# Values after the output rows in a local attention, and two PSUM rings in a second attention

## The chip, the cores and the metric

The kernel runs on one core of one Trainium2 chip. The metric is the device time of one execution, in microseconds. A core has five engines that run their own instruction streams and meet at semaphores: TensorE (PE: matrix products), VectorE (DVE), ScalarE (ACT), GpSimd (POOL) and SyncE (SP, which issues DMAs here). Products land in PSUM banks, and another engine has to read a bank before TensorE may form the next product in it.

## The reference

Four blocks in a row, each added to its input after a normalisation. x is 16 x 512 x 128, fp32; 8192 rows in all.

```python
x = x + _layernorm(_L0_attn_ref(_layernorm(x), w_qkv, w_out))       # local attention
x = x + _layernorm(_L0_ffn_ref(_layernorm(x), centroids, ...))      # routing, 8 experts
x = x + _layernorm(_L1_attn_ref(_layernorm(x), Wqkv, bqkv, Wout, bout))
x = x + _layernorm(_L1_ffn_ref(_layernorm(x), W1, b1, ...))

# _L0_attn_ref: 16 heads of 64, window of 32
xn = x * rsqrt(mean(x * x) + 1e-6)
q, k, v = split(xn @ w_qkv.T)
q, k = apply_rope(q), apply_rope(k)
mask = (q_pos >= k_pos) & (q_pos - k_pos <= 32)
out = softmax(where(mask, q @ k.T / 8, -1e9)) @ v @ w_out.T

# _L1_attn_ref: 16 heads of 8, all 512 positions
q, k, v = split(x @ Wqkv + bqkv)
q, k = apply_rope(q), apply_rope(k)
out = softmax(q @ k.T / sqrt(8)) @ v @ Wout + bout
```

## The kernel before

The program is a chain of stages that each cover the whole input, with every engine's instructions written out in order and semaphores between them. The change touches two stages: `l0_attention` and `l1_attention`. The time axis of the trace has the local attention up to about 1083 us, then routing, the expert layer, the second attention from about 1650 to 2660 us, and the last layer.

**Local attention.** A batch (512 rows) is 8 steps, numbered s = 0 to 7, one for each pair of heads (128 of the 1024 inner dimensions), 16 batches, 128 steps. In each step TensorE forms the projections of queries and keys for the pair (`project`, L540, three passes each, as the fp32 operands are split in a high and a low part) and one piece of the values of a coming batch (`value`, L530), from two `a_proj` banks used in turn; then the scores of the pair (`max_scores` and the shifted, turned ones, L578 to L621), and for older pairs the sums of the exponentials (L634), the weighted values (L643) and the rows of the output (`rows`, L548). Sums, reciprocal and rows work on four heads at once, so they come once in two steps: sums at the end of an odd step, rows at the start of an even one. ScalarE copies each projection out (`a_raw`, L352, and `a_v`, L334), VectorE multiplies queries and keys by the cosines (`a_qT`, `a_kT`, L477), GpSimd multiplies the swapped copy by the sines (L303) and adds (L308). VectorE also takes maxima of the scores (L493), the reciprocal of the sums (L509) and the scaling by it (L483, L514).

A bank may be written again when the semaphore `copied` says that ScalarE has read it; for values and queries the kernel also waits for `rope_done`, a count of VectorE's products. The list `uses` sets which bank each use gets. Once a batch, fixed by step offsets (LOAD_X to SUM_Y), come the statistics of the next input, its factor, its normalisation (`normalised`, L414), its turning by TensorE (`transposes`, L524), and the same for the output (`OUT_Y`, L445, and sums). The factor of a normalisation, 1/sqrt(variance + 1e-5) followed by the rms one, is formed on GpSimd by seven small operations on 128 x 4 (`factors`, `sum_factors`).

**Second attention.** One batch is a turn of 32 steps, 16 turns. Each step has one unit of scores for maxima (two matmuls, L1955, read by VectorE's `reduce_max`, L1759) and one of turned, shifted scores (two matmuls, L1973, read by ScalarE's exponential, L1688). Beside these, at fixed steps (`SLOTS`), a turn has twelve other products: `turn_in` (the normalised input turned, read by ScalarE, L1698), `q0` to `q3` (queries and keys and their swapped copies, L1916, read by VectorE, which adds the bias and multiplies by cosine or sine in one operation, L1771), `v` (L1921, bias added by VectorE, L1778), `out0` to `out3` (read by VectorE, `quotients`), `att` (L1935, read by ScalarE) and `y` (bias added by VectorE). These twelve share a ring of two double banks, `s_ps`, with the scores for maxima; the turned scores have three banks of their own, `t_ps`. GpSimd adds two products to rotated queries or keys (`wholes`, L1619).

## Time and profile before

| | |
|---|---|
| median of 3 runs | 2857.4 us (2855.66 to 2862.07) |
| the profiled execution | 2855.56 us, its span 2853.8 us |
| TensorE busy | 2106.2 us (74%) |
| VectorE busy | 2078.9 us (73%) |
| ScalarE busy | 1500.5 us (53%) |
| GpSimd busy | 1161.3 us (41%) |
| mean granted TensorE clock | 0.877 of full |

The busy shares are means over five stages. In each stage the stretch views below give the shares of that stage, and a single instruction that comes once per pair of steps or once per turn (first start, last start, count) gives the length of a pair or a turn. A timeline shows one pair, with the idle time ahead of an instruction and what ended it in square brackets.

### The profile page before, as it was taken

The numbers are of one execution on the slowest core, as the hardware profiler recorded it, in microseconds if no ns is written. First come the engines' busy times: TensorE is split into PE (matmuls) and PEld (weight loads), VectorE is DVE, ScalarE is ACT, GpSimd is POOL, SyncE is SP. The second block draws the span as 40 slices with busy tenths as digits, with TensorE's granted clock in tenths as the row PEclk, the third lists the DMA queues.
The fourth block names the chain that finished last, engine by engine and source line by source line (L and its number), as shares of the span: only waits on it lengthen the run. The fifth ranks groups of instructions, "written<-read, shape, count | busy, mean of one in ns | idle before, by whom it ended". The sixth has DMA issues, their size and how long they took to land. (4 is left out here: it accounts for less than half of the span.)

```text
span 2853.8 us, 73730 instructions
## 1 busy us (share of the span) xinstructions
PE 2106.2 (74%) x26748; PEld 1206.3 (42%) x26748; DVE 2078.9 (73%) x5353; ACT 1500.5 (53%) x2776; POOL 1161.3 (41%) x1165
## 2 busy tenths in 40 slices
PE   4898989888989987111009828888888888888597
PEld 3676767666767766100004302222322222232354
DVE  4677777776767775766417828888888888888598
ACT  4565656565656652000005406666666666667487
POOL 5677667676767770000363346311221112210122
PEclk9999999999999996555559958998999999999799
DMA  3233333332333330000022233311122111120001
GB/s 103 65 82 72 73 75 74 79 77 70 74 75 76 75 70 6 1 1 1 21 69 68 77 64 59 51 27 24 24 30 37 28 24 23 29 39 4 9 26 33
DMA packets 103685, 136.76 MB, mean 48 GB/s; under 512 B 23782, under 2 KB 78982, under 8 KB 103047
## 3 DMA queue, kind: packets, MB, share of 16 engines
q1 hardware_dynamic: 99206, 123.34, 19.6%
q0 software_dynamic: 4096, 8.40, 1.1%
q8 instruction: 232, 3.80, 0.6%
q14 instruction: 151, 1.23, 0.2%
HBM read 26.52 MB, written 12.58 MB: 14 GB/s over the span
## 5 line engine op out<-in xcount | busy, mean ns | idle before, releaser
L1759 DVE TENSOR_REDUCE d_nmax_<-d_s_ 128x2 bf16<-128x1024 f32 x512 | 619.9, 1223 | 116.3 <-PE d_s_ L1955 113.7
L1688 ACT ACTIVATE d_pT_<-d_t_ 128x512 f32<-128x512 f32 x1024 | 557.1, 598 | 243.7 <-PE d_t_ L1973 235.7
L303 POOL TENSOR_TENSOR a_other<-a_other,a_rope 128x512 f32<-128x512 f32 x256 | 322.1, 1279 | 300.6 <-DMA a_other<-a_raw 300.4
L1986 PE MATMUL d_o_<-d_pT_,d_v_ 128*32 128x256 f32 x4096 | 332.3, 410 | 0.2 <-ACT d_pT_ L1688 0.2
L1973 PE MATMUL d_t_<-d_qs_,d_ks_ 49*128 49x512 bf16 x1024 | 207.5, 402 | 84.2 <-ACT d_pT_ L1688 42.4
L371 ACT ACTIVATE a_pT<-a_t 64x384 f32<-64x384 f32 x512 | 248.2, 485 | 33.2 <-PE a_t L621 23.9
L509 DVE RECIPROCAL a_rden<-a_o 128x512 f32<-128x512 f32 x64 | 214.5, 3352 | 52.7 <-PE a_o L634 52.7
L1955 PE MATMUL d_s_<-d_ks_,d_qs_ 48*128 48x512 bf16 x1024 | 208.0, 403 | 58.3 <-DMA d_ks_<-d_part_ 29.0
L477 DVE TENSOR_TENSOR a_qT<-a_proj,a_rope 128x512 f32<-128x512 f32 x128 | 87.6, 684 | 165.4 <-ACT a_raw L352 165.3
L1188 ACT ACTIVATE c_hT_<-c_in_,c_beta_,c_gamma_ 128x512 f32<-128x512 f32 x16 | 12.4, 777 | 359.2 <-PE c_in_ L1308 359.2
L823 POOL DMA_INDIRECT sorted_x<-x_tokens,pos x64 | 61.5, 961 | 313.8 <-DVEq L720 294.6
L352 ACT COPY a_raw<-a_proj 128x512 f32<-128x512 f32 x256 | 150.6, 588 | 73.4 <-PE a_proj L540 68.7
L540 PE MATMUL a_proj<-a_xnT_hi,a_w_lo 128*128 128x512 f32 x256 | 116.8, 456 | 93.9 <-ACT a_v L334 88.0
L1973 PEld LDWEIGHTS d_t_<-d_qs_,d_ks_ 49*128 49x128 bf16 x1024 | 49.7, 93 | 316.4 <-ACT d_pT_ L1688 203.5
L358 ACT CAST a_qB<-a_qT 128x512 bf16<-128x512 f32 x128 | 79.3, 620 | 184.9 <-POOL a_qT L308 184.8
L877 PE MATMUL b_tot<-b_count,b_ones 128*128 128x3 bf16 x126 | 23.6, 187 | 201.1 <-DVE b_junk L959 189.3
L643 PE MATMUL a_o<-a_pT,a_v 128*32 128x160 f32 (+1 forms) x4096 | 168.4, 306 | 4.1 <-DVE a_oT L514 2.4
L308 POOL TENSOR_TENSOR a_kT<-a_kT,a_other 128x512 f32<-128x512 f32 x128 | 164.1, 1282 | 0.0
L308 POOL TENSOR_TENSOR a_qT<-a_qT,a_other 128x512 f32<-128x512 f32 x128 | 163.6, 1278 | 0.0
L1986 PEld LDWEIGHTS d_o_<-d_pT_,d_v_ 128*32 128x32 f32 x4096 | 90.5, 111 | 172.6 <-ACT d_pT_ L1688 90.9
L548 PE MATMUL a_y<-a_wo,a_oT 128*128 128x128 f32 x1024 | 135.2, 287 | 17.2 <-issue 16.4
L643 PEld LDWEIGHTS a_o<-a_pT,a_v 128*32 128x32 f32 x4096 | 123.9, 113 | 37.1 <-issue 21.4
(269 smaller groups left out, 4695.6 us busy)
## 6 DMA issues: line engine op xcount, KB each, us to landing
a_other<-a_raw SPq DMA_DIRECT2D x512, 128.0 KB, 2.4
d_qs_<-d_part_ SPq DMA_DIRECT2D x192, 64.0 KB
d_ks_<-d_part_ SPq DMA_DIRECT2D x192, 64.0 KB
a_xpre<-x SPq DMA_DIRECT2D x16, 256.0 KB, 2.8
a_xres<-x SPq DMA_DIRECT2D x16, 256.0 KB, 2.9
c_xs_<-sorted_x SPq DMA_DIRECT2D x16, 256.0 KB, 2.7
c_w_<-e_w SPq DMA_DIRECT2D x16, 256.0 KB, 3.2
sorted_x<-c_xs_ SPq DMA_DIRECT2D x16, 256.0 KB, 2.0
```

The lines of the kernel that those rows point to most:

```text
L303: nc.gpsimd.tensor_tensor(other[s % 2][:, side, :], other[s % 2][:, side, :], rope[:, 1, :], ALU.mult).then_inc(rope2_done, 1)
L308: nc.gpsimd.tensor_tensor(dst, dst, other[s % 2][:, side, :], ALU.add).then_inc(add_done, 1)
L352: nc.scalar.copy(raw[s % 2][:, side, :], proj[bank][:, 0:T]).then_inc(copied, 1)
L371: nc.scalar.activation(dst[rows, :, 64 * c:64 * c + HB], src[rows], ACT.Exp, scale=SCALE).then_inc(exp_done, 1)
L509: nc.vector.reciprocal(rden[:], o_ps[:, 0:T]).then_inc(rden_done, 1)
L548: ins = nc.tensor.matmul(y_ps[:, t * 128:(t + 1) * 128], oT[:, 2 * (chunk % 2) + half, t * 128:(t + 1) * 128], wo_sb[:, 2 * chunk + half, ...
L643: ins = nc.tensor.matmul(o_ps[QD * i:QD * (i + 1), 128 * t:128 * t + widths[t]], v_sb[k_v][:, t, col:col + QD], pT[k_p][i][:, BAND * t:BAN ...
L1688: nc.scalar.activation(pT[kt][pair][:, a, :], t_ps[(j + turn.k) % 3][:], ACT.Exp).then_inc(exp_done, 1)
L1759: nc.vector.reduce_max(out, bank_of(unit, e)[:], AX_X, negate=True).then_inc(read_dve, 1)
L1955: nc.tensor.matmul(bank_of(unit, e)[:, a, :], qs[e.k][rows, hp, qt * 128:(qt + 1) * 128], ks[e.k][rows, hp, :], start=True, stop=True).the ...
L1973: nc.tensor.matmul(t_ps[(2 * n + a + e.k) % 3][:], ks[e.k][rows, hp, kt * 128:(kt + 1) * 128], qs[e.k][rows, hp, :], start=True, stop=True ...
L1986: ins = nc.tensor.matmul(o_ps[HC * i:HC * (i + 1), cols], v[e.k][:, kt, g * GH + i, :], pT[kt][i // 2][:, i % 2, cols], start=(kt, half) = ...
```

## The change

**Local attention.** The order of a step on TensorE becomes queries, keys, (turned input), rows or the rest of the weighted values, values, scores; it was rows, values, queries, keys, (turned input), rest, scores. The banks of queries, keys and values follow this order in `uses`, and the bank of values now waits for the count of VectorE's products of the same step. The values of the next batch begin a step later (`V_FIRST`), the steps of loading, normalising and turning move by one, and each factor is one power on GpSimd of a number that VectorE forms from the variance with one multiply-add.

```diff
-        NCONST = 6 + 8
+        NCONST = 4 + 8
...
-        LOAD_X, STAT_X, NORM_X, TURN_X, LOW_X = -12, -8, -6, -5, -4
-        LOAD_RES, COPY_Y, STAT_Y, OUT_Y, SUM_Y = 10, 14, 15, 17, 18
-        V_FIRST = 5
+        LOAD_X, STAT_X, ROOT_X, NORM_X, TURN_X, LOW_X = -11, -8, -7, -5, -4, -3
+        LOAD_RES, COPY_Y, STAT_Y, ROOT_Y, OUT_Y, SUM_Y, ROOT_SUM = 10, 14, 15, 16, 17, 18, 19
+        V_FIRST = 6
...
-            uses += [("v", s), ("q", s), ("k", s)]
+            uses += [("q", s), ("k", s)]
             if s == TURN_X % PAIRS:
                 uses += [("xn", s)]
+            uses += [("v", s)]
...
-                n = 6 * b
                 pool.wait_ge(stats1, b + 1)
-                nc.gpsimd.tensor_tensor(ve[:], mv1[:, :, 1], eps5[:], ALU.add).then_inc(pool_step, 1)
...
-                nc.gpsimd.tensor_tensor(comb[:], rr[:], rstd[:], ALU.mult).then_inc(comb_ready, 1)
+                nc.gpsimd.tensor_tensor(comb[:], ve[:], neg_half[:], ALU.pow).then_inc(comb_ready, 1)
...
+                ins.then_inc(x_stat, 1)
+                dve.wait_ge(x_stat, 2 * b + 2)
+                nc.vector.tensor_scalar(ve[:], mv1[:, :, 1], 1.0 + 1e-6, 1e-11, ALU.mult, ALU.add).then_inc(stats1, 1)
...
-                products = 2 * (PAIRS * b + s) + (1 if what == "xn" else 0)
-                if what != "k" and (before or what == "xn"):
-                    pe.wait_ge(rope_done, products)
+                ready = {"q": 0, "k": None, "xn": 1, "v": 2 if s == TURN_X % PAIRS else 1}[what]
+                if ready is not None and (before or ready):
+                    pe.wait_ge(rope_done, 2 * (PAIRS * b + s) + ready)
...
+                if alive(0, before, left):
+                    if s == 0:
+                        pe.wait_ge(xnT_ready, b + 1)
+                    for side, what in enumerate("qk"):
+                        bank = bank_of(b, k, s, what, before, left)
+                        project(k, s, side, bank)
+                if s == TURN_X % PAIRS and formed("xn", s, left):
+                    transposes(b + 1, bank_of(b, k, s, "xn", before, left))
                 if s % 2 == 0 and alive(LAG_ROWS, before, left):
...
+                if s % 2 == 1 and alive(LAG_REST, before, left):
+                    quad, chunk = quad_of(b, s, LAG_REST)
+                    pe.wait_ge(norm_done, 2 * quad + 1)
+                    weighted_values(chunk, k if s >= LAG_REST else 1 - k, chunk % 2, 1)
                 if formed("v", s, left):
...
-                    value(kv, nv, bank)
...
+                    value(kv, nv, bank, scores_next)
```

On TensorE, an even step in the middle of the local attention, from the sums of one four-head group (`a_ones`) to the first scores. Before (`a_w_lo,a_xnT_hi` is the values' product, `a_xnT_hi,a_w_lo` a query's or key's):

```order
L634 MATMUL a_o<-a_pT,a_ones 32x128 x4
L548 MATMUL a_y<-a_wo,a_oT 128x128 [waits a_norm_done]
L548 MATMUL a_y<-a_wo,a_oT 128x128 x7
L530 MATMUL a_proj<-a_w_lo,a_xnT_hi 128x512 [waits a_rope_done,a_copied]
L530 MATMUL a_proj<-a_w_hi,a_xnT_lo 128x512
L530 MATMUL a_proj<-a_w_hi,a_xnT_hi 128x512
L540 MATMUL a_proj<-a_xnT_hi,a_w_lo 128x512 [waits a_rope_done,a_copied]
L540 MATMUL a_proj<-a_xnT_lo,a_w_hi 128x512
L540 MATMUL a_proj<-a_xnT_hi,a_w_hi 128x512
L540 MATMUL a_proj<-a_xnT_hi,a_w_lo 128x512 [waits a_copied]
L540 MATMUL a_proj<-a_xnT_lo,a_w_hi 128x512
L540 MATMUL a_proj<-a_xnT_hi,a_w_hi 128x512 [waits a_exp_done,a_max_done,a_round_done]
```

The same place now:

```order
L601 MATMUL a_o<-a_pT,a_ones 32x128 x4
L507 MATMUL a_proj<-a_xnT_hi,a_w_lo 128x512 [waits a_rope_done,a_copied,a_xnT_ready]
L507 MATMUL a_proj<-a_xnT_lo,a_w_hi 128x512
L507 MATMUL a_proj<-a_xnT_hi,a_w_hi 128x512
L507 MATMUL a_proj<-a_xnT_hi,a_w_lo 128x512 [waits a_copied]
L507 MATMUL a_proj<-a_xnT_lo,a_w_hi 128x512
L507 MATMUL a_proj<-a_xnT_hi,a_w_hi 128x512
L515 MATMUL a_y<-a_wo,a_oT 128x128 [waits a_norm_done]
L515 MATMUL a_y<-a_wo,a_oT 128x128 x7
L499 MATMUL a_proj<-a_w_lo,a_xnT_hi 128x512 [waits a_rope_done,a_copied]
L499 MATMUL a_proj<-a_w_hi,a_xnT_lo 128x512
L499 MATMUL a_proj<-a_w_hi,a_xnT_hi 128x512 [waits a_exp_done,a_max_done,a_round_done]
```

Queries and keys moved to right behind the sums, the rows behind them, and the values, which wait for `a_rope_done`, are last ahead of the scores.

On VectorE, the normalisation of the next input (`a_xpre`) among the maxima (`a_nmax`) and the reciprocal. Before:

```order
L477 TENSOR_TENSOR a_qT<-a_proj,a_rope 128x512 [waits a_copied]
L476 REGISTER_ALU
L477 TENSOR_TENSOR a_kT<-a_proj,a_rope 128x512 [waits a_copied]
L492 ISA [waits a_st_done]
L493 TENSOR_REDUCE a_nmax<-a_s 128x4 [waits a_s_done]
L492 REGISTER_ALU
L493 TENSOR_REDUCE a_nmax<-a_s 128x4 [waits a_s_done]
L414 TENSOR_SCALAR a_xpre<-a_xpre,a_mv,a_comb 128x128 [waits a_comb_ready]
L414 TENSOR_SCALAR a_xpre<-a_xpre,a_mv,a_comb 128x128 x3
```

The same operation now:

```order
L460 TENSOR_REDUCE a_nmax<-a_s 128x4 [waits a_s_done]
L381 TENSOR_SCALAR a_xpre<-a_xpre,a_mv,a_comb 128x128 [waits a_comb_ready]
L381 TENSOR_SCALAR a_xpre<-a_xpre,a_mv,a_comb 128x128 x3
L475 REGISTER_ALU [waits a_den_done]
L476 RECIPROCAL a_rden<-a_o 128x512 [waits a_norm_done]
L443 REGISTER_ALU [waits a_st_done]
L444 TENSOR_TENSOR a_qT<-a_proj,a_rope 128x512 [waits a_copied]
```

The normalisation moved from an even step, where no reciprocal follows in the step, to an odd one, where the reciprocal and the product of the queries stand directly behind it.

**Second attention.** The shared ring is split by reader. `s_ps` keeps the scores for maxima and `out0` to `out3`, which VectorE reads; `t_ps`, three banks, takes the turned scores and `turn_in`, `q0` to `q3`, `v`, `att` and `y`, which ScalarE reads. ScalarE adds the bias to queries and keys as it reads; GpSimd multiplies by cosine or sine and adds the biases of the values and of the output. The places of the twelve products in the turn change.

```diff
-    SLOTS = (("turn_in", -42), ("q0", -41), ("q1", -40), ("q2", -38), ("q3", -37), ("v", -23),
-             ("out0", 13), ("out1", 21), ("out2", 29), ("out3", 37), ("att", 41), ("y", 44))
...
-    FIRST_PART, SECOND_PART = (-37, -34), (-33, -31)
-    WHOLE, REST, THIRD_PART = (-40, -37), (-36, -35), (-34, -33)
...
+    FOR_ACT = {"turn_in": -46, "q0": -45, "q1": -44, "q2": -43, "q3": -42, "v": -28, "att": 41, "y": 44}
+    FOR_DVE = {"out0": 13, "out1": 21, "out2": 29, "out3": 37}
+    ROPE = (-44, -43, -42, -41)
+    FIRST_PART, SECOND_PART = (-40, -37), (-36, -35)
...
+    BIAS_V, BIAS_Y = -27, 45
...
-    STAT_Y, STAT_Y2, ROOT_Y, NORM_Y, NORM_Y2, ADD_Y = 47, 48, 51, 60, 62, 63
+    STAT_Y, STAT_Y2, ROOT_Y, NORM_Y, NORM_Y2, ADD_Y = 48, 49, 51, 56, 59, 63
...
+            def rope_product(e, c):
+                pool.wait_ge(t_read, t_done_by(f"q{c}", e))
+                nc.gpsimd.tensor_tensor(prod[:, c, :], prod[:, c, :], rope[:, c, :], ALU.mult).then_inc(roped, 1)
...
+            def biased_values(e):
...
+            def biased_output(e):
...
+            def read(what, e):
...
+                    nc.scalar.activation(prod[:, c, :], bank[:], ACT.Identity, bias=bqk[:, c:c + 1]).then_inc(t_read, 1)
...
-                nc.vector.scalar_tensor_tensor(prod[:, c, :], bank_of(what, e)[:, 0, :], bqk[:, c:c + 1], rope[:, c, :],
-                                               ALU.add, ALU.mult).then_inc(read_dve, 1)
...
+            def s_room(what, e):
...
+                    pe.wait_ge(s_read, place - 1)
...
+            def t_room(what, e):
...
+                    pe.wait_ge(t_read, place - 2)
```

On VectorE, the second attention where queries and keys are formed; `d_prod_` is the product with cosine or sine. Before:

```order
L1771 SCALAR_TENSOR_TENSOR d_prod_<-d_s_,d_bqk_,d_rope_ 128x512 [waits d_formed,d_whole_ready]
L1759 TENSOR_REDUCE d_nmax_<-d_s_ 128x2 [waits d_formed]
L1771 SCALAR_TENSOR_TENSOR d_prod_<-d_s_,d_bqk_,d_rope_ 128x512 [waits d_formed]
L1759 TENSOR_REDUCE d_nmax_<-d_s_ 128x2 [waits d_formed] x2
L1764 STREAM_TRANSPOSE d_nmaxT_<-d_nmax_ 128x32 [waits d_read_dve,d_shifts_in0]
L1771 SCALAR_TENSOR_TENSOR d_prod_<-d_s_,d_bqk_,d_rope_ 128x512 [waits d_formed,d_whole_ready]
L1759 TENSOR_REDUCE d_nmax_<-d_s_ 128x2 [waits d_formed]
L1771 SCALAR_TENSOR_TENSOR d_prod_<-d_s_,d_bqk_,d_rope_ 128x512 [waits d_formed]
```

The reads now stand on ScalarE, between the exponentials (`d_pT_0_`, `d_pT_1_`):

```order
L1713 ACTIVATE d_prod_<-d_t_,d_bqk_ 128x512 [waits d_whole_ready,d_t_formed]
L1699 ACTIVATE d_pT_0_<-d_t_ 128x512 [waits d_t_formed,d_av_done]
L1699 ACTIVATE d_pT_0_<-d_t_ 128x512 [waits d_t_formed]
L1713 ACTIVATE d_prod_<-d_t_,d_bqk_ 128x512 [waits d_t_formed]
L1699 ACTIVATE d_pT_1_<-d_t_ 128x512 [waits d_t_formed] x2
L1713 ACTIVATE d_prod_<-d_t_,d_bqk_ 128x512 [waits d_whole_ready,d_t_formed]
L1699 ACTIVATE d_pT_0_<-d_t_ 128x512 [waits d_t_formed,d_av_done]
L1699 ACTIVATE d_pT_0_<-d_t_ 128x512 [waits d_t_formed]
L1713 ACTIVATE d_prod_<-d_t_,d_bqk_ 128x512 [waits d_t_formed]
```

Four reads in four steps in a row, each behind two exponentials, in place of four VectorE operations among maxima in five steps.

## Rows read from the trace of the kernel before

**Rows 1.** Busy us of PE, PEld, DVE, ACT, POOL; PEclk, DMA, GB/s.

```profile
70.00:1083.00 1013.00, 905.10 (x17931) 698.47 (x17923) 729.00 (x1267) 609.35 (x1154) 715.40 (x710) 0.97 0.31 73
...
1740.00:2600.00 860.00, 722.12 (x6304) 247.53 (x6300) 748.71 (x1289) 574.35 (x1080) 193.29 (x175) 0.94 0.19 31
```

**Rows 2.** Reciprocal of the sums, line 509: duration ns, first and last start.

```profile
L509 DVE RECIPROCAL a_rden<-a_o x64: 3339/3356/3359, 70.5 to 1083.3; 128x512 f32<-128x512 f32 x64
```

**Rows 3.** Waits, 100 to 1050 us: engine, line, awaited: us, times, longest.

```profile
PE a_proj L540 <- ACT a_v L334: 74.2, 58, 3.0
```

**Rows 4.** Timeline, one pair of steps: start, us, what, [idle before <-releaser].

```profile
511.66 1.24 PE L634 MATMUL a_o<-a_pT,a_ones 128*32 128x160 f32 x32
...
512.83 2.05 PE L548 MATMUL a_y<-a_wo,a_oT 128*128 128x128 f32 x16
...
513.06 3.36 DVE L509 RECIPROCAL a_rden<-a_o 128x512 f32<-128x512 f32 x1 [1.47 <-PE a_o L634]
...
514.64 0.48 PE L530 MATMUL a_proj<-a_w_lo,a_xnT_hi 128*128 128x512 f32 x1
...
516.26 0.50 PE L540 MATMUL a_proj<-a_xnT_hi,a_w_lo 128*128 128x512 f32 x1
...
516.93 0.69 DVE L477 TENSOR_TENSOR a_qT<-a_proj,a_rope 128x512 f32<-128x512 f32 x1 [0.52 <-ACT a_raw L352]
...
517.14 0.36 PE L578 MATMUL a_s<-a_mq,a_identb 64*64 64x384 bf16 x4
...
518.98 1.24 PE L643 MATMUL a_o<-a_pT,a_v 128*32 128x160 f32 x32
...
520.15 0.51 PE L530 MATMUL a_proj<-a_w_lo,a_xnT_hi 128*128 128x512 f32 x1
...
525.69 1.24 PE L634 MATMUL a_o<-a_pT,a_ones 128*32 128x160 f32 x32
```

**Rows 5.** Timeline, the step with the turned rows, local attention.

```profile
505.35 0.50 PE L540 MATMUL a_proj<-a_xnT_hi,a_w_lo 128*128 128x512 f32 x1 [2.48 <-ACT a_v L334]
...
506.66 1.11 PE L524 MATMUL a_proj<-a_ident,a_xpre 128*128 128x128 f32 x4 [0.36 <-DVE a_qT L477]
```

**Rows 6.** Groups of instructions, local attention: busy us, mean ns | idle.

```profile
L303 POOL TENSOR_TENSOR a_other<-a_other,a_rope 128x512 f32<-128x512 f32 x256 | 322.1, 1279 | 300.6 <-DMA a_other<-a_raw 300.4
...
L414 DVE TENSOR_SCALAR a_xpre<-a_xpre,a_mv,a_comb 128x128 f32<-128x128 f32 x64 | 41.4, 772 | 3.7 <-POOL a_comb L272 3.7
...
L445 DVE TENSOR_SCALAR a_ysb<-a_ysb,a_mv,a_rstd 128x128 f32<-128x128 f32 x64 | 39.1, 670 | 1.1 <-POOL a_rstd L313 1.1
```

**Rows 7.** Turning copy of the second attention, line 1698.

```profile
L1698 ACT COPY d_zT_<-d_s_ x16: 586/586/592, 1661.4 to 2532.6; 128x512 f32<-128x512 f32 x16
```

**Rows 8.** Groups of instructions, second attention and a like activation.

```profile
L1771 DVE SCALAR_TENSOR_TENSOR d_prod_<-d_s_,d_bqk_,d_rope_ 128x512 f32<-128x512 f32 x64 | 47.4, 741 | 9.7 <-PE d_s_ L1916 9.6
...
L2210 ACT ACTIVATE e_turns_<-e_h_,e_offset_ 128x512 f32<-128x512 f32 x64 | 44.3, 692 | 11.0 <-PE e_h_ L2355 11.0
```

**Rows 9.** Values add, line 1778, by its tile.

```profile
L1778 DVE TENSOR_TENSOR d_v_<-d_s_,d_bv_ x16: 678/691/692, 1669.3 to 2567.5; 128x512 f32<-128x512 f32 x16
```

**Rows 10.** Timeline, a projection step, then the step of the values.

```profile
2057.24 0.39 PE L1973 MATMUL d_t_<-d_qs_,d_ks_ 49*128 49x512 bf16 x2
...
2057.78 1.12 PE L1916 MATMUL d_s_<-d_zT_,d_wqk_ 128*128 128x512 f32 x2
...
2059.40 0.39 PE L1973 MATMUL d_t_<-d_qs_,d_ks_ 49*128 49x512 bf16 x2
...
2089.70 1.16 PE L1921 MATMUL d_s_<-d_wv_,d_zT_ 128*128 128x128 f32 x8 [1.23 <-DVE d_nmax_ L1759]
...
2091.22 0.66 PE L1935 MATMUL d_s_<-d_ident_,d_att_ 128*128 128x128 f32 x4 [0.36 <-DVE d_nmax_ L1759]
```

**Rows 11.** Waits, 1800 to 2600 us.

```profile
DVE d_nmax_ L1759 <- PE d_s_ L1955: 85.0, 109, 2.5
```

**Rows 12.** Output rows, line 1808: duration ns min/median/max.

```profile
L1808 DVE TENSOR_SCALAR d_yn_<-d_yb_,d_mv_,d_rstd_ x64: 333/390/1202, 1830.8 to 2657.5; 128x128 f32<-128x128 f32 x64
```

More of the change, by code:

```diff
@@ L1692, in step @@
                     exponentials(turn, n)
-                e = of(turn, n, SLOT_STEP["turn_in"])
-                if e is not None:
-                    act.wait_ge(formed, formed_by("turn_in", e))
-                    if not (isinstance(e.n, int) and e.n < 1):
-                        act.wait_ge(formed, formed_by("v", earlier(e)))
-                    nc.scalar.copy(zT[:], bank_of("turn_in", e)[:, 0, :]).then_inc(read_act, 1)
+                for what in due(FOR_ACT, n):
+                    e = of(turn, n, FOR_ACT[what])
+                    if e is not None:
+                        read(what, e)
                 for g in range(NG):
```

390 lines of the change are left out of this document (174 added, 216 removed).

## The prediction

> **What bounds the kernel now.** I read the page first (busy shares, slices, costliest groups), then the stretches by engine, the waits, and timelines of a few steps. The span is 2853.8 us and the profiled run took 2855.56 us; the median of the runs is 2857.4 us, 1.8 us more. The change touches two stages, the local attention and the second attention. In neither is an engine full [rows 1]: local attention has TensorE busy 905 of 1013 us, VectorE 729, GpSimd 715, ScalarE 609; second attention has VectorE busy 749 of 860 and TensorE 722. At such shares the time is set by chains between engines, so the order of the instructions decides.
>
> *Local attention.* One reciprocal of 3.36 us per pair of steps is a pacemaker that can be counted [rows 2]: 64 of them, first start 70.5, last 1083.3, so (1083.3 - 70.5)/63 = 16.08 us a pair and 64.3 us a batch of eight steps. An undisturbed pair [rows 4] takes 525.69 - 511.66 = 14.03 us, 56.1 a batch, and in it TensorE has no gap: sums, rows of the output, values, queries and keys follow each other, while the reciprocal runs beside them. So a batch loses 64.3 - 56.1 = 8.2 us somewhere. The waits name 5.0 of it: queries or keys wait for ScalarE's copy of the values 58 times, 74.2 us in 950 [rows 3], that is 74.2/950 x 64.3 = 5.0. The other 3.2 us are the turned rows (1.11 [rows 5]) and small things.
>
> *Second attention.* One copy per turn paces it [rows 7]: (2532.6 - 1661.4)/15 = 58.08 us a turn. Scaled to a turn, VectorE is busy 748.7/860 x 58.08 = 50.6 us, TensorE 48.8, ScalarE 38.8, GpSimd 13.1. VectorE leads and waits only for scores from TensorE, 85.0 us in 109 waits [rows 11]; TensorE in turn waits for VectorE to empty the shared ring (1.23 and 0.36 us) [rows 10].
>
> **Part 1, local attention: values after rows, keys free of the values' copy.** What goes: keys no longer wait for the copy of the values of the same step. At most the 5.0 us a batch. What comes: the values' bank now waits for VectorE's product of the queries of the same step, and on VectorE that product stands behind the reciprocal in each even step. The chain of an even step, with the durations of [rows 4], from the start of the sums:
> sums to reciprocal 513.06 - 511.66 = 1.40, reciprocal 3.36, product 0.69, and 0.1 that I add for two hand-overs: 5.55 us.
> TensorE gets to the values earlier than that: sums 512.83 - 511.66 = 1.17; two projections take 1.62 (514.64 to 516.26); rows 514.64 - 512.83 = 1.81; together 4.60. It waits 0.95 us, then values 0.88 (516.26 to 517.14), scores 1.84 (to 518.98), head 1.17 (to 520.15), and the odd step 5.54 (to 525.69), in which the product is early enough (projection, copy, product about 2.3 us, against 2.8 of work ahead of the values). The pair is 5.55 + 0.88 + 1.84 + 1.17 + 5.54 = 14.98 us, four of them 59.9.
>
> What stands ahead of a reciprocal on VectorE now lengthens the chain, where until now TensorE's own work hid it. In two pairs of a batch something does:
> - the normalised output, in the program's step 1: 4 x 0.670 [rows 6] + 0.69 for the residual add (a 512-wide two-input operation like the product of [rows 4]) + 0.2 = 3.6; VectorE's 1.47 us of idle ahead of the reciprocal [rows 4] absorb their part: +2.1.
> - the normalised input, moved from step 2 to step 3, and so from behind a reciprocal to right ahead of the next: 4 x 0.772 [rows 6] - 1.47 = +1.6.
> - the turned rows, moved from step 3 to step 4, an even one. They wait for the same product, and the 1.11 us of the transposes [rows 5] and the 1.81 of the rows, which filled the wait before, now come behind it: +2.9.
> A batch: 59.9 + 2.1 + 1.6 + 2.9 = 66.5 us, against 64.3. If the small leftovers of before stay (3.2 less the 1.1 that I have just counted), 68.6. There are 126 steps, 15.75 batches: (66.5 - 64.3) x 15.75 = +35 to (68.6 - 64.3) x 15.75 = +68. I take +45, nearer the low end, as the waits on the values' copy took part of the leftovers with them. The other end: if the first two additions are swallowed by other gaps a batch is 62.8, -24. The 14.03 us pair would be worth 5.0 x 15.75 = -79, but the diff's order excludes it.
>
> **Part 2, factors in one power each.** GpSimd loses 12 instructions of 128x4 per batch, VectorE gains 2 of that size. The factors are wanted a step later than they are formed, GpSimd is busy 71% [rows 1] with the two-input operations of 1.279 us [rows 6], and nobody on the chain waits for it: 0. If the cover went, VectorE's small instructions (two per batch) would add well under 1 us a batch.
>
> **Part 3, second attention.** VectorE loses per turn four products at 0.741 [rows 8] and two bias adds at 0.69 [rows 9]: 4.34 us, 65 us over 15 turns if all comes back. Not all does. The four products fall in steps that TensorE sets: with the projection in it a step is 2059.40 - 2057.24 = 2.16 us [rows 10], against 58.08/32 = 1.82 for the mean one, and the four projections now stand in consecutive steps and still cost TensorE 1.12 each. I give nothing for these 3.0 us. The two adds (1.4) come back, and with the rings apart, a bit over half of the waits of 1.23 and 0.36 [rows 10]: 0.9. Together 2.3 a turn, 15 turns: -35. Bounds: 1.4 (-21) and 4.34 (-65).
> ScalarE takes four reads of 0.692 [rows 8] and two copies of 0.586 [rows 7]: 38.8 + 3.9 = 42.7 of some 56 us; in a projection's step two exponentials (about 0.6 each, as the copy) and one read make 1.9 us, under 2.16, so a ring of three banks is emptied in time: 0. If it weren't, each of eight insertions would wait one read, 8 x 0.586 = 4.7 us a turn, with the scores and so all of VectorE's maxima queued behind. GpSimd takes four products and two adds of 1.279: 13.1 + 7.7 = 20.8 us a turn. The rotated rows come some 5 us later and are asked for 3 to 4 steps earlier: 0.
>
> **A rule that speaks against it.** One 128x128 operation of VectorE, the normalised output rows of the second attention, takes 333 ns at best, 390 in the median and 1202 at worst [rows 12], and its like in the local attention, where GpSimd is five times as busy, 670 and 772 on average [rows 6]. The trace shows by this that something beside it stretches it. The Trainium skill, "SBUF — State Buffer", section "Who interferes with whom", says that such a VectorE instruction takes a port pair that it shares with GpSimd, and that whoever comes first holds it for a whole instruction. By that rule the six new GpSimd operations would stretch VectorE's work beside them; the trace agrees as far as the spread goes.
>
> **The rivals.**
> A, the forecast: 2855.6 + 45 - 35 = 2865.6, and 1.8 to the median, 2867. Own range, with the bounds above: +35 - 65 to +68 - 21, 2827 to 2904. For it: the reciprocal's place is fixed by the order. 0.44.
> B, faster: the additions ahead of the reciprocals don't bite, as the lost 8.2 us a batch came from ScalarE's copies and TensorE catches up in the pairs between. Local attention -24, second attention -35: 2798; with all of VectorE's 4.34 us back, 2768. It decides where the reciprocal is not what the values wait for. For it: 5.0 us a batch of named waits [rows 3]; against: 14.98 is above 14.03 in every pair. 0.34.
> C, slower: the second attention gives nothing, since the rows of the output, four a turn, go from 0.39 to 1.20 us [rows 12], 3.2 us a turn or 49 us in all, more than the 35: 2855.6 + 45 + 1.8 = 2902. Against: these rows lie far from the rotations in the order. 0.10.
> D: the two parts cancel, or the first is nothing and the second too: 2857 within 0.2%, 5.7 us, about what a measurement of this kernel can tell from no change. 0.12.
>
> **The numbers.** Faster: B and 0.03 of A's low end, 0.37. Same: D and 0.03 of A, 0.15. Slower: the rest of A, 0.38, and C, 0.10, 0.48. The range goes from between B's two values, 2785, to C, 2905.
>
> **What would show it.** Right: the 64 reciprocals' starts 66 to 69 us apart per eight steps; on TensorE a wait at the values for VectorE's product of about 1 us in even steps, about 3 after the normalised output, and the turned rows waiting as long; turns of about 55.8 us, VectorE's busy time in the second attention some 69 us less (16 x 4.34). Wrong: reciprocals under 64.3 us per batch (B), no wait of the values for the product, turns above 57.5 us with longer output rows (C), or TensorE waiting for ScalarE's reads in the three-bank ring.

## The result, and the profile after

The changed kernel takes 2751.8 us in the median of 4 runs (2741.57 to 2757.0), the kernel before 2856.5 on the same chip; the ratio is 0.962 (95% interval 0.959 to 0.965). The forecast was 2867 us, slower, with a range down to 2785: it was wrong in sign and the time lies outside the range. The span of the profiled run fell from 2853.8 to 2748.7 us, by 105.1 us. The single instructions that pace a stage say where it went. After, with the reciprocal of the local attention, the first and last operations of the routing, and the turning copy of the second attention:

```profile
L476 DVE RECIPROCAL a_rden<-a_o x64: 3343/3357/3359, 59.0 to 1066.2; 128x512 f32<-128x512 f32 x64
...
L883 DVE TENSOR_SCALAR b_zz<-x_tokens,mean,comb x64: 337/342/348, 1085.2 to 1123.0; 128x128 f32 x48, 128x128 f32<-128x128 f32 x16
...
L990 DVE CAST pos<-b_place x1: 195/195/195, 1347.0 to 1347.0; 128x64 int32<-128x64 f32 x1
...
L1708 ACT COPY d_zT_<-d_t_ x16: 585/593/594, 1611.5 to 2421.1; 128x512 f32<-128x512 f32 x16
```

Before, the two of the routing, which the prediction had not looked at (the others are in [rows 2] and [rows 7]):

```profile
L916 DVE TENSOR_SCALAR b_zz<-x_tokens,mean,comb x64: 336/341/348, 1104.4 to 1142.3; 128x128 f32 x48, 128x128 f32<-128x128 f32 x16
...
L1023 DVE CAST pos<-b_place x1: 195/195/195, 1397.1 to 1397.1; 128x64 int32<-128x64 f32 x1
```

| stretch | before | after | difference |
|---|---|---|---|
| start to the first reciprocal | 70.5 | 59.0 | -11.5 |
| 63 pairs of the local attention | 1012.8 | 1007.2 | -5.6 |
| last reciprocal to first b_zz | 21.1 | 19.0 | -2.1 |
| routing, first b_zz to pos | 292.7 | 261.8 | -30.9 |
| pos to the first turning copy | 264.3 | 264.5 | +0.2 |
| 15 turns of the second attention | 871.2 | 809.6 | -61.6 |
| last turning copy to the end | 321.2 | 327.6 | +6.4 |

The last two belong together: the turning copy stands four steps earlier in its turn. Of the 61.6 us, 12.3 are in the first turn (42.7 to 30.4 us), none in turns 2 and 3 (114.7 and 114.9 us together), 49.5 in the last 12 (59.5 to 55.4 us each). Against the forecast the three parts are: local attention +45 forecast, -19 measured (start, pairs and the way to the routing); second attention -35 and -55; routing not counted and -31. The biggest surprise is the routing, whose code the change does not touch. The busy times of the two attentions after, in the same columns as [rows 1]:

```profile
59.00:1066.00 1007.00, 891.44 (x17918) 703.30 (x17918) 713.66 (x1296) 605.86 (x1155) 657.89 (x536) 0.98 0.32 74
1690.00:2500.00 810.00, 694.09 (x6302) 230.85 (x6300) 691.22 (x1196) 621.84 (x1163) 296.32 (x257) 0.96 0.21 33
```

A turn (55.7 us, mean of the last 14) has 691.2/810 x 55.7 = 47.5 us of VectorE, 4.0 less than before by the same working, 42.8 of ScalarE (42.7 was forecast) and 20.4 of GpSimd (20.8 was forecast). An undisturbed even step of the local attention after, TensorE and VectorE:

```profile
594.35 1.24 PE L601 MATMUL a_o<-a_pT,a_ones 128*32 128x160 f32 x32
595.52 0.50 PE L507 MATMUL a_proj<-a_xnT_hi,a_w_lo 128*128 128x512 f32 x1
595.75 3.36 DVE L476 RECIPROCAL a_rden<-a_o 128x512 f32<-128x512 f32 x1 [0.79 <-PE a_o L601]
...
597.01 1.95 PE L515 MATMUL a_y<-a_wo,a_oT 128*128 128x128 f32 x16
...
599.02 0.63 DVE L444 TENSOR_TENSOR a_qT<-a_proj,a_rope 128x512 f32<-128x512 f32 x1
...
599.71 0.50 PE L499 MATMUL a_proj<-a_w_lo,a_xnT_hi 128*128 128x512 f32 x1 [0.75 <-DVE a_qT L444]
```

From the sums to the values are 599.71 - 594.35 = 5.36 us (5.55 forecast), the values wait 0.75 us for VectorE's product behind the reciprocal (0.95 forecast), and the first pair of a batch, which nothing disturbs, is 14.75 us in nearly every batch (14.98). The chain is as forecast. What it costs a batch is not.

### The profile page after: what moved, and what is told of

Read it like the earlier page. It is cut to its first block and busy times, and to the rows that moved or that the text cites. A ratio compares the mean times of both kernels' runs of the same rounds, so it can differ in the third digit from the quotient of the medians.

```text
span 2748.7 us, 73587 instructions
## 1 busy us (share of the span) xinstructions
PE 2061.8 (75%) x26748; PEld 1195.5 (43%) x26748; DVE 1992.3 (72%) x5289; ACT 1552.3 (56%) x2872; POOL 1218.4 (44%) x1067
## 5 line engine op out<-in xcount | busy, mean ns | idle before, releaser
L1975 PE MATMUL d_o_<-d_pT_,d_v_ 128*32 128x256 f32 x4096 | 326.3, 403 | 0.2 <-ACT d_pT_ L1699 0.2
L1962 PE MATMUL d_t_<-d_qs_,d_ks_ 49*128 49x512 bf16 x1024 | 207.7, 402 | 86.8 <-ACT d_pT_ L1699 41.6
L476 DVE RECIPROCAL a_rden<-a_o 128x512 f32<-128x512 f32 x64 | 214.7, 3355 | 49.5 <-PE a_o L601 49.4
L299 ACT COPY a_v<-a_proj 128x512 f32<-128x512 f32 x128 | 74.9, 585 | 278.8 <-PE a_proj L499 278.8
L460 DVE TENSOR_REDUCE a_nmax<-a_s 128x4 bf16<-128x384 f32 x256 | 130.7, 552 | 134.7 <-PE a_s L565 134.3
L610 PE MATMUL a_o<-a_pT,a_v 128*32 128x160 f32 (+1 forms) x4096 | 160.6, 296 | 12.7 <-DVE a_oT L481 9.5
L515 PEld LDWEIGHTS a_y<-a_wo,a_oT 128*128 128x128 f32 x1024 | 133.6, 206 | 5.9 <-DVE a_oT L450 1.1
```

What stands on the lines that cost most here:

```text
L476: nc.vector.reciprocal(rden[:], o_ps[:, 0:T]).then_inc(rden_done, 1)
L515: ins = nc.tensor.matmul(y_ps[:, t * 128:(t + 1) * 128], oT[:, 2 * (chunk % 2) + half, t * 128:(t + 1) * 128], wo_sb[:, 2 * chunk + half, ...
L610: ins = nc.tensor.matmul(o_ps[QD * i:QD * (i + 1), 128 * t:128 * t + widths[t]], v_sb[k_v][:, t, col:col + QD], pT[k_p][i][:, BAND * t:BAN ...
L1962: nc.tensor.matmul(t_bank(2 * n + a, e)[:], ks[e.k][rows, hp, kt * 128:(kt + 1) * 128], qs[e.k][rows, hp, :], start=True, stop=True).then_ ...
L1975: ins = nc.tensor.matmul(o_ps[HC * i:HC * (i + 1), cols], v[e.k][:, kt, g * GH + i, :], pT[kt][i // 2][:, i % 2, cols], start=(kt, half) = ...
```

## The experiments

The runs were on several chips, on which the kernel before takes 2857 to 2902 us. So totals are compared as ratios to the kernel before on the same chip, and stages by the instructions above. "Pairs" are means over the 63 pairs of the local attention. The same code gives stages that differ between profiles: the changed local attention has 15.92 to 16.24 us a pair in seven of them, the changed second attention 55.7 to 58.1 us a turn in nine (the shortest in the first comparison). A difference within such a spread shows nothing.

The profiles in parts, in us. A middle batch is the mean of the second to the 14th batch of the local attention; routing is first `b_zz` to `pos`; turns are between turning copies; the last column is TensorE's mean granted clock in the last 12 turns, as a share of full.

| run | middle batch | routing | first turn | turns 2 + 3 | each of the last 12 | clock there |
|---|---|---|---|---|---|---|
| before | 65.3 | 292.7 | 42.7 | 114.7 | 59.5 | 0.93 |
| changed | 65.4 | 261.8 | 30.4 | 114.9 | 55.4 | 0.97 |
| e1 | 66.0 | 292.6 | 30.7 | 135.8 | 55.9 | 0.96 |
| e2 | 65.9 | 261.8 | 41.6 | 156.9 | 59.0 | 0.94 |
| e3 | 63.0 | 261.9 | 42.1 | 157.3 | 59.3 | 0.94 |
| e4 | 66.2 | 261.5 | 41.6 | 156.8 | 58.8 | 0.94 |
| e5 | 63.6 | 261.8 | 30.6 | 139.6 | 55.1 | 0.97 |
| e6 | 64.1 | 292.4 | 42.9 | 154.4 | 59.3 | 0.94 |
| e7 | 65.4 | 261.8 | 39.3 | 155.5 | 59.3 | 0.94 |
| e8 | 62.8 | 261.7 | 30.7 | 132.4 | 55.1 | 0.97 |
| e9 | 65.1 | 261.7 | 30.7 | 134.0 | 55.9 | 0.95 |
| e10 | 61.9 | 261.9 | 30.7 | 133.2 | 56.2 | 0.95 |
| e11 | 65.9 | 261.7 | 28.8 | 133.9 | 59.2 | 0.92 |
| e12 | 65.8 | 261.7 | 27.9 | 141.3 | 58.8 | 0.92 |
| e13 | 66.7 | 261.5 | 30.4 | 136.0 | 56.4 | 0.95 |
| e14 | 68.6 | 261.7 | 30.3 | 135.9 | 56.1 | 0.94 |
| e15 | 66.1 | 288.6 | 30.7 | 113.2 | 56.4 | 0.95 |

Two things in it bear on all that follows. First, the chips differ almost only in turns 2 and 3: about 115 us for either code in before, changed and e15, 154 to 157 (old code) and 132 to 141 (new) in all the others. There TensorE, VectorE and ScalarE stand still together, for up to 18 us at a time, as here in e9, where the profile calls the releaser `remote` and names no instruction:

```profile
1749.79 1.23 DVE L1788 TENSOR_REDUCE d_nmax_<-d_s_ 128x2 bf16<-128x1024 f32 x1 [16.72 <-remote]
```

What it is stays open. Second, the granted clock of the last 12 turns differs with the code. Among single turns of these twelve, over all profiles, that were granted 0.94 the old code takes 58.8 us on average and the new 56.8; among those at 0.97, 58.2 and 55.4. So 2.0 to 2.8 us a turn are there at an equal clock, and the rest of the 3 to 4 comes together with a higher clock; what raised the clock no run here separates.

**e1: the second attention alone.** Edit: the kernel before with `l1_attention` of the change.

> The kernel before with the second attention of the change alone; local attention and routing as before. Theory: the second attention gives 3.5 us a turn and some 12 us in its first turn, less 6 us at its end: 2856.5 - 49 - 12 + 6 = 2801 us, and the routing (first b_zz to the cast of pos) stays at 293 us, the local attention at 16.08 us a pair. Rival: the gain of the second attention comes from what the stages ahead of it left (clock, earlier loads): then it would be under 20 us here.

Measured 2829.9 us, ratio 0.974 (0.971 to 0.977). Local attention 16.23 us a pair, routing 292.6 us. Against the old code on the same chip (e2 to e4) the first turn is 11 us shorter, turns 2 and 3 about 21 together, each of the last 12 by 2.9 to 3.4 us. All of it comes from the second attention itself. The whole is 4.2 us a turn over 14 turns, but that mean mixes the standstills of turns 2 and 3 with the steady turns.

**e2: the local attention alone.** Edit: the kernel before with `l0_attention` of the change.

> The kernel before with the local attention of the change alone. Theory: first reciprocal 11.5 us earlier, 63 pairs 5.6 us shorter, routing (its code unchanged) 31 us shorter: about 2806 us. Rival (what was forecast): the values' wait costs 2.2 us a batch or more and the routing does not change: 2890 us or more.

Measured 2851.5 us, ratio 0.983 (0.979 to 0.987); pairs 16.10 us, routing 261.8. Of the 48 us, 31 are the routing. A middle batch (65.9) is as long as with the old code (66.0 and 66.2 in e1 and e4): what the local attention itself gained lies at its start and in its first batch.

**e3: the factors alone.** Edit: one power per factor in the kernel before, on a variance that VectorE has multiplied and added to; order and offsets stay.

```diff
-                nc.gpsimd.tensor_tensor(ve[:], mv1[:, :, 1], eps5[:], ALU.add).then_inc(pool_step, 1)
...
-                nc.gpsimd.tensor_tensor(comb[:], rr[:], rstd[:], ALU.mult).then_inc(comb_ready, 1)
+                nc.gpsimd.tensor_tensor(comb[:], ve[:], neg_half[:], ALU.pow).then_inc(comb_ready, 1)
```

> The kernel before with only the factors of the local attention as one power each (12 fewer GpSimd operations of 128x4 a batch, two more of VectorE); the order of the steps stays. Its VectorE program stands 14 instructions further on at the routing's expert loop, as in the changed kernel. Theory A (the place of the loop in the instruction memory decides): routing 262 us instead of 293, the start 5.5 us earlier, pairs still 16.1 us: 2820 us. Rival B (the order of the steps brought the whole 31 + 11.5 us): no change, 2856 us. By what was forecast (zero) 2857 us.

Measured 2819.0 us, ratio 0.971 (0.968 to 0.973): 81 us, and 32 us better than the whole new local attention. Routing 261.9. The miss: the pairs fell too, to 15.57 us. I had costed this edit at nothing. GpSimd's part of the chains of before, by line, 100 to 1050 us (busy us, mean ns):

```profile
L262 POOL TENSOR_TENSOR a_rstd<-a_ve,a_neg_half 128x4 f32<-128x4 f32 x14 | 14.2, 1017 | 1.1
L279 POOL TENSOR_TENSOR a_rstd<-a_ve,a_neg_half 128x4 f32<-128x4 f32 x14 | 14.2, 1017 | 1.1
L287 POOL TENSOR_TENSOR a_rr<-a_ms,a_neg_half 128x4 f32<-128x4 f32 x14 | 14.1, 1007 | 1.2 <-POOL a_ms L285 0.2
L270 POOL TENSOR_TENSOR a_rr<-a_ms,a_neg_half 128x4 f32<-128x4 f32 x14 | 14.1, 1006 | 1.1
...
L281 POOL TENSOR_TENSOR a_ms<-a_rstd 128x4 f32<-128x4 f32 x14 | 2.8, 201 | 1.1
```

A power of 128x4 takes 1.01 us, five times the other small operations. Two chains a batch are 4 x 1.01 + 10 x 0.21 = 6.1 us of GpSimd and 2.0 after. TensorE's wait for ScalarE's copy of the values, 74.2 us in [rows 3], is here:

```profile
PE a_proj L514 <- ACT a_v L306: 45.1, 55, 1.8
```

That is 29.1/950 x 64.3 = 2.0 us a batch, of the 3 by which a middle batch is shorter than in e4. Nearly all of it is in the third pair of a batch, where the wait falls from 3.2 to 1.1 us. There, before, a chain of seven stands ahead of GpSimd's rotations (its last operation is the first line here); ScalarE's cast of the rotated queries waits for these, and the copy of the values, for which TensorE waits 2.48 us [rows 5], stands behind the cast:

```profile
496.97 0.20 POOL L272 TENSOR_TENSOR a_comb<-a_rr,a_rstd 128x4 f32<-128x4 f32 x1
497.12 2.53 POOL L303 TENSOR_TENSOR a_other<-a_other,a_rope 128x512 f32<-128x512 f32 x2
499.61 1.27 POOL L308 TENSOR_TENSOR a_qT<-a_qT,a_other 128x512 f32<-128x512 f32 x1
500.91 0.62 ACT L358 CAST a_qB<-a_qT 128x512 bf16<-128x512 f32 x1 [2.34 <-POOL a_qT L308]
...
504.71 0.59 ACT L334 COPY a_v<-a_proj 128x512 f32<-128x512 f32 x1
```

**e4: 20 idle instructions ahead of the routing.** Edit, in the kernel before:

```diff
+            for u in range(20):
+                nc.vector.memset(spare[:, u:u + 1], 0.0)
```

> The kernel before with 20 idle 128x1 memsets on VectorE ahead of the routing, so that its expert loop (220 instructions) stands 20 instructions further on. No data changes. Theory A (a loop body that lies across a border of the instruction blocks waits for its code each time round): the 5.3 us gap at the end of each of seven experts falls to 0.5, routing 262 to 264 us, total 2827 us. Rival B (the new factors' values or the state left by the stage ahead brought it): routing 293 us and 1 us for the memsets, 2858 us.

Measured 2866.3 us, ratio 0.988 (0.984 to 0.991), 33 us faster with more work in it. The routing takes 261.5 us. So the routing's 31 us can be had with neither new data nor a new order. VectorE between two experts, before and after (start, us, idle ahead in brackets):

```profile
1216.64 0.15 DVE L1016 TENSOR_SCALAR b_base<-b_base 128x1 f32<-128x1 f32 x1
1222.10 0.22 DVE L993 TENSOR_TENSOR b_a<-b_hi,b_free 128x64 f32<-128x64 f32 x1 [5.32 <-issue]
```

```profile
1192.05 0.15 DVE L983 TENSOR_SCALAR b_base<-b_base 128x1 f32<-128x1 f32 x1
1192.70 0.23 DVE L960 TENSOR_TENSOR b_a<-b_hi,b_free 128x64 f32<-128x64 f32 x1 [0.51 <-DVE b_base L983]
```

Before, the engine stands still for 5.32 us at the loop's branch back, waiting for nothing that the profile shows; after, for 0.51. There are six such places, 5.2 to 5.7 us each before and 0.51 to 0.54 after: 29 to 30 of the 31 us.

**e5: factors and second attention, without the new order.** Edit: e3 with `l1_attention` of the change.

> The local attention of the kernel before with only the factors changed (e3) and the second attention of the change: the changed kernel without its new order of rows, keys and values. Theory (the new order costs time, the factors and the second attention bring it): pairs 15.57 us against 16.10 with the new order on one chip (e3, e2), 33 us less than the changed kernel, so about 0.962 - 33/2856 = 0.950 of the kernel before. Rival (order and factors only work together with the second attention, or the chip's state made e2 slow): 0.962 or more.

Measured 2745.1 us, ratio 0.946 (0.944 to 0.948), pairs 15.66 us. Against 0.955 for the changed kernel on a like chip (e9) the new order costs about 25 us.

**e6: the new order with the old chains.** Edit: e2 with the seven-operation chains put back.

> The kernel before with the new order and step offsets of the local attention, but the old chains of seven GpSimd operations for the factors. Forecast of the prediction for this part alone: +35 to +68 us, pairs 16.6 to 17.1 us. Rival: in the new order ScalarE no longer stands between GpSimd and TensorE, the chains cost little, pairs stay near the 16.10 of e2: 0 to +10 us. The expert loop of the routing stands where it stood in the kernel before, so the routing takes 293 us in both cases.

Measured 2870.0 us, ratio 0.989 (0.988 to 0.991), pairs 15.76 us, routing 292.4. The order alone makes the kernel faster by 29 us: my +45 us for it is refuted, and so is the rival's 0 to +10. Order and factors take away the same wait: the queries or keys waiting for ScalarE's copy of the values, itself behind GpSimd (75 us from 100 to 1050 us in e4, 45 in e3, none in e6 and e2). And within the new order the new factors cost time: a middle batch is 64.1 us with the old chains (e6) and 65.9 with the new factors (e2, on another chip).

**e7: idle powers.** Edit, in e3, two ahead of each factor:

```diff
+                for u in range(2):
+                    nc.gpsimd.tensor_tensor(idle[:], ve[:], neg_half[:], ALU.pow).then_inc(idle_step, 1)
+                    pool.wait_ge(idle_step, 2 * b + u + 1)
```

> The kernel of e3 with two idle powers of 128x4 on GpSimd ahead of each of the two factors a batch, four in all, some 4.2 us of GpSimd, as much as the change of the factors took away; their output is not used, all data is as in e3. Theory (the time of the factors came through GpSimd's queue, where the rotated queries and then ScalarE's copy of the values stand behind them): pairs back from 15.6 to 16.2 us, and TensorE's wait for the copy of the values back from 45 to 75 us. Rival (it came because the factor was there earlier or as VectorE's normalisations were stretched less often): pairs under 15.8.

Measured 2851.8 us, ratio 0.983 (0.981 to 0.985), pairs 16.04 us, and the wait is back:

```profile
PE a_proj L523 <- ACT a_v L315: 74.3, 60, 2.9
```

So the time that the chains take in GpSimd's queue is enough to account for e3's gain. The idle powers also hold the factor itself back, so e7 alone does not separate the queue from the factor's arrival; but no normalisation waits for its factor from 100 to 1050 us, in before, e3 or e7 (0.0 us of idle time). What e7 leaves open is the share of the normalised input, which is stretched along with the chains: 0.63 us an operation in before, 0.35 in e3, 0.59 in e7.

**e8: rows ahead of the transposes.** Edit, in the changed kernel:

```diff
-                if s == TURN_X % PAIRS and formed("xn", s, left):
-                    transposes(b + 1, bank_of(b, k, s, "xn", before, left))
                 if s % 2 == 0 and alive(LAG_ROWS, before, left):
...
                     rows(quad, chunk)
+                if s == TURN_X % PAIRS and formed("xn", s, left):
+                    transposes(b + 1, bank_of(b, k, s, "xn", before, left))
```

> The changed kernel, but in the step that turns the next input TensorE does the rows of the output ahead of the transposes, which wait for VectorE's product of the queries. Theory (the step of the prediction that gave +2.9 us a batch; measured 2.2): 1.8 us less a batch, up to 28 us, ratio to before 0.953. Rival (the wait is given back in the next pairs): 0.962.

Measured 2731.9 us, ratio 0.9445 (0.942 to 0.947). The pair with the turned rows falls from 17.9 us (e9) and 18.3 (e2) to 15.6, pairs 15.44 on average. It is about 30 us better than the changed kernel on a like chip (0.9547, e9).

**e9: the changed kernel again**, on a chip like those of the experiments.

> The changed kernel itself, on the chip of the experiments, whose kernel before takes 2898 us where the first comparison had 2857. If the stages add up as e1 and e2 have them: pairs 16.1 us, turns 57.4 us, ratio 0.950 to 0.956. If the first comparison carries over as a ratio: 0.962.

Measured 2767.4 us, ratio 0.955 (0.953 to 0.957), pairs 15.92, turns 57.5 us. The ratio depends on the chip (0.962 in the first comparison), and the table shows where: turns 2 and 3 of the old code take 40 to 43 us more here than there, those of the changed code 19 more.

**e10: the variance's factor on GpSimd.** Edit, in e8 (with 20 idle memsets as in e4):

```diff
-                nc.vector.tensor_scalar(ve[:], mv1[:, :, 1], 1.0 + 1e-6, 1e-11, ALU.mult, ALU.add).then_inc(stats1, 1)
...
+                nc.gpsimd.tensor_tensor(ve[:], mv1[:, :, 1], scale6[:], ALU.mult).then_inc(scaled, 1)
+                pool.wait_ge(scaled, b + 1)
```

> e8 (rows ahead of the transposes) with the multiply-add of the variance, two operations of 128x4 a batch on VectorE, replaced by a multiplication of 128x4 on GpSimd ahead of each power; 20 idle memsets on VectorE keep the routing's expert loop where it stood. Theory (those VectorE operations take 0.8 to 1.2 us in place of 0.17, as GpSimd's 1.28 us ones hold them up, ahead of the scaling of the values): 1.5 to 2 us less a batch, pairs 15.0 to 15.1 against 15.44, 20 us faster than e8, ratio 0.938. Rival (they are hidden): 0.9445 as e8.

Measured 2736.1 us, ratio 0.9447 (0.943 to 0.947): no gain in the total. In the profiles the local attention is 11 us shorter (pairs 15.26), the untouched second attention 14 us longer, within its own spread. So the theory is seen in the stage and not in the time. The 0.9 us by which a middle batch is shorter (62.8 to 61.9) are in its third pair (15.7 to 14.9). The operations that it took away (L434 and L376) and one that stayed, in e2:

```profile
L434 DVE TENSOR_SCALAR a_ve<-a_mv 128x4 f32<-128x4 f32 x14 | 16.3, 1162 | 0.0
L376 DVE TENSOR_SCALAR a_ve<-a_mv 128x4 f32<-128x4 f32 x13 | 10.2, 785 | 0.8
...
L407 DVE TENSOR_SCALAR a_ve<-a_mv 128x4 f32<-128x4 f32 x14 | 2.9, 205 | 0.5
```

**e11 and e12: GpSimd's new work of the second attention on VectorE.** Edits, in the changed kernel: the four multiplications (e11), and the two bias adds too (e12).

```diff
-                nc.gpsimd.tensor_tensor(prod[:, c, :], prod[:, c, :], rope[:, c, :], ALU.mult).then_inc(roped, 1)
+                nc.vector.tensor_tensor(prod[:, c, :], prod[:, c, :], rope[:, c, :], ALU.mult).then_inc(roped, 1)
```

> The changed kernel with the four multiplications by cosine or sine of a turn on VectorE in place of GpSimd; rings, reads by ScalarE and bias adds as in the change. VectorE gets back 4 x 0.69 = 2.8 us a turn. Theory of the prediction (the four lie in steps that TensorE sets and cost nothing there): turns as in the changed kernel on this chip (e9). Rival (VectorE's work of a turn is what counts, wherever it stands): 2.8 us a turn more, 39 us over 14 turns.

> As e11, and the two bias adds (values, output) on VectorE too, 4.2 us a turn in all; what is left of the change in the second attention is then the split of the ring and ScalarE's reads. If VectorE's work decides: turns 4.2 us longer than the changed kernel's, 59 us in all, about those of the kernel before. If the split of the ring brought most of it: under 2 us a turn longer.

e11 measured 2818.2 us, ratio 0.9725 (0.9705 to 0.9745), turns 60.3 us; e12 2818.4 us, 0.9727 (0.971 to 0.9745), turns 60.5 us. The turning copy in e9, e11 and e12, of which the turns are read (less the first one):

```profile
L1708 ACT COPY d_zT_<-d_t_ x16: 586/586/592, 1606.0 to 2441.6; 128x512 f32<-128x512 f32 x16
```

```profile
L1706 ACT COPY d_zT_<-d_t_ x16: 586/592/592, 1618.4 to 2491.4; 128x512 f32<-128x512 f32 x16
```

```profile
L1687 ACT COPY d_zT_<-d_t_ x16: 586/590/592, 1619.2 to 2493.9; 128x512 f32<-128x512 f32 x16
```

In the last 12 turns the four multiplications on VectorE cost 59.2 - 55.9 = 3.3 us a turn against their 4 x 0.69 = 2.8; 1.2 if turns of an equal clock, 0.94, are compared (58.1 in four turns of e11, 56.8 for the changed code). VectorE is busy 47.9 us of a turn in e9, 51.3 in e11, 52.1 in e12 and 51.9 in e2 to e4, and idle for 8.0, 7.9, 6.6 and about 7 us: the turn grows nearly by what VectorE is given. The two adds cost nothing (58.8 against 59.2 us, equal totals), where 1.4 was forecast. What is left between e12 and the old code in these turns is 0.0 to 0.5 us; the split ring and the moved steps show in turns 2 and 3 (141 against 154 to 157 us) and in the first one (28 against 39 to 43). Of the 51 us that e11 is above e9, 37 are turns and 11 the local attention, whose code is the same (16.09 against 15.92 us a pair).

**e13 and e15: 50 and 110 idle memsets in the changed kernel**, in the place of e4.

> The changed kernel with 50 idle 128x1 memsets on VectorE ahead of the routing; no data changes. Theory (the expert loop's 220 instructions now lie across a border of 256 again): the 0.5 us between two experts goes back to 5.3, the routing from 262 to 294 us, about 34 us slower than the changed kernel (ratio 0.966 against 0.955). Rival (the loop is quick in the changed kernel for another reason, such as its new data): 3 us slower at most.

> The changed kernel with 110 idle 128x1 memsets on VectorE ahead of the routing (e13 had 50, and the expert loop stayed quick). If borders of 256 instructions decide and the loop's first instruction stood close behind one, 110 put a border well inside the loop of 220: the gap between two experts 5.3 us, the routing 292 to 296 us. If the loop stays quick here too (262 us), the place in the instruction memory is not shown to be what decides, and e4 has another cause.

e13 measured 2798.9 us, ratio 0.9635 (0.960 to 0.967), routing 261.5 us: my theory was wrong for 50, and the routing is no part of what it has above e9 (pairs 16.24 and turns 58.1 us; chip or padding, not settled). e15 measured 2798.8 us, ratio 0.979 (0.975 to 0.982), on a chip like the first one; its routing takes 288.6 us, and the standstills are back (six, of 4.9 to 5.4 us), now in two pieces:

```profile
1178.97 0.23 DVE L963 TENSOR_TENSOR b_a<-b_hi,b_free 128x64 f32<-128x64 f32 x1 [3.03 <-issue]
...
1181.28 0.28 DVE L929 TENSOR_SCALAR_CACHE_REDUCE b_junk<-b_a,b_tries 128x64 f32<-128x64 f32 x1 [1.88 <-issue]
```

**e14: the turned rows a step earlier.** Edit, in the changed kernel:

```diff
-        LOAD_X, STAT_X, ROOT_X, NORM_X, TURN_X, LOW_X = -11, -8, -7, -5, -4, -3
+        LOAD_X, STAT_X, ROOT_X, NORM_X, TURN_X, LOW_X = -11, -8, -7, -6, -5, -4
```

> The changed kernel with the turned input back in step 3, an odd one (and its second part in step 4), rows order as in the change. The transposes then wait for a product that has no reciprocal ahead of it. Theory: the fourth pair of a batch falls from 17.5 to 18.5 us to about 15 to 15.6 as in e8, but the normalised input, which now has to be there half a step after VectorE's reciprocal, may come late: the third pair up by 0 to 1 us; pairs 15.3 to 15.6 us, ratio 0.944 to 0.950. Rival (the wait only moves): pairs 15.9, ratio 0.955.

Measured 2827.0 us, ratio 0.973 (0.970 to 0.976), pairs 16.70 us: the opposite of the theory. The fourth pair did fall (14.75 us), but the third rose to 22.3, from 15.9 (e2). The normalisation of the input, in e14 and then in e8 (min, median, max ns):

```profile
L381 DVE TENSOR_SCALAR a_xpre<-a_xpre,a_mv,a_comb x64: 336/1302/1334, 6.3 to 993.9; 128x128 f32<-128x128 f32 x64
```

```profile
L381 DVE TENSOR_SCALAR a_xpre<-a_xpre,a_mv,a_comb x64: 328/341/4636, 6.3 to 923.1; 128x128 f32<-128x128 f32 x64
```

One step earlier it lies among GpSimd's rotations, and each of four takes 1.30 us in place of 0.34, which is also its median in the changed kernel (e9). The next product of the queries, for which the transposes wait, is behind them.

## Why the prediction was wrong

**Step "factors in one power each: 0" failed.** It was costed without reading GpSimd's rows. They showed 1.01 us for a power. And "nobody on the chain waits for it" was wrong: GpSimd's queue was on the chain (rotated queries, ScalarE's cast of them, its copy of the values, the bank of the keys). e3 gives 81 us less 31 for the routing, about 50 us, with the old order; e7 takes most of it back. In the new order, where that wait is gone, the same edit costs time (e6 against e2), by VectorE's two small operations, which the prediction put at "well under 1 us a batch": taking them away gives 0.9 (e10 against e8).

**Step "values wait for the product: +2.2 to +4.3 us a batch" failed in its sum, not in its chain.** The wait (0.75 us) and the undisturbed pair (14.75 us) are as worked out. But a middle batch takes 65.4 us after and 65.3 before, +0.1. From the forecast 66.5 to 65.4, term by term:

- Four undisturbed pairs are 59.0 us, not 59.9.
- The normalised output costs 0.3 us (15.05 against 14.75 in e2), not 2.1. It was taken at 4 x 0.67 [rows 6], which was right for its place before: four in a row take 1.1 to 3.8 us there, 2.4 on average. Moved with the new order, they take 1.11 in 14 of 16 batches, and 1.11 + 0.69 - 1.47 = 0.33:

```profile
428.38 3.07 DVE L445 TENSOR_SCALAR a_ysb<-a_ysb,a_mv,a_rstd 128x128 f32<-128x128 f32 x4
```

```profile
608.83 1.11 DVE L412 TENSOR_SCALAR a_ysb<-a_ysb,a_mv,a_rstd 128x128 f32<-128x128 f32 x4
```

- The third pair, with the normalised input, is 1.2 us above 14.75, not 1.6. But the input too fell to 1.11 us for four, which the idle time ahead of the reciprocal would hold: with the old chains (e6) the pair is 0.4 above, and 0.2 in e10 against 1.0 in e8. By these, most of the 1.2 is the multiply-add of the variance.
- The turned rows cost 3.1 us on average (2.2 or 3.9 in most batches), 2.9 forecast; e8 gives back 2.3 to 2.7 of them.
- Not in the sum: every second batch the loop of 16 steps turns, and TensorE stands for 3.4 to 4.2 us at its start, before and after, waiting for nothing that the profile shows. That is 1.8 us a batch of the 8.2 that the prediction searched for, and no order changes it.

The 64.3 us of before, too, were a mean with the shorter end of the stage in it. Alone, the order is a gain of 29 us (e6), beside the new factors a loss of 32 us (e3 against e2): it takes away the wait that the factors had already made short, and adds the wait behind the reciprocal.

**Step "the four products lie in steps that TensorE sets: nothing" failed in size.** 2.3 us a turn were forecast; the last 12 turns are 4.1 us shorter in the first comparison and 2.9 to 3.4 in e1, as much as VectorE lost. The step was judged by one step of 2.16 us [rows 10]. e11 shows that the four are not free, and e12 that in the last 12 turns the adds, which were counted in full, are. How much of it is VectorE's work and how much the higher clock that goes with it (0.93 or 0.94 to 0.95 or 0.97) stays open; at an equal clock 2.0 to 2.8 us a turn are left. The first turn's 12 us, the queries' way to the first scores, was not counted at all.

**Rival C did not happen.** The 64 output rows of the second attention average 0.55 us after and 0.54 before, though a stretch by GpSimd is seen elsewhere. The Trainium skill, "SBUF — State Buffer", section "Who interferes with whom", has one side lock out the other for a whole instruction: e14's 0.34 to 1.30 us, with GpSimd's operations at 1.28, agree with it. The place of an operation beside GpSimd's decides, not how much GpSimd does in total.

**The routing was left out**, as its code is the same. e4 shows that 20 idle instructions ahead make its loop 31 us quicker, e15 that 110 in the changed kernel make it slow again. The Trainium skill, "Runtime: NRT & Kernel Launch", section "Instruction fetch mechanics", says that an engine holds two blocks of 256 instructions, fetched in sequence, and that a branch back out of them waits for a fetch. The loop has 220 instructions on VectorE. Counted from its place in the kernel before (slow), it begins 14 instructions later in e3 (quick), 20 in e4 (quick), 64 in e13 (quick) and 124 in e15 (slow). A border that lies 1 to 14 instructions behind the loop's old beginning, and the next 256 further, fits all but e13, whose last 14 to 27 instructions would lie behind the next one without a standstill. So it is shown that instructions ahead of the loop switch the standstill on and off, and the blocks are a reading that one run of five does not fit. Where the borders are, and how far a loop may reach past one, stays open.

Rival B had the right sign, and without the routing nearly the sizes (-24 and -35 to -65 us for the two parts, -19 and -55 measured). That is mostly luck: its condition, that the reciprocal is not what the values wait for, did not hold, and the addition that did not bite was small because it moved away from GpSimd's operations.
